# Causal attention and a routed expert layer on one core: masks of one-head score pieces moved from TensorE to VectorE, and the pieces dealt anew among half units

## What is computed

```python
Q, K, V = (proj_split(w, bias) for w, bias in ((q_w, q_b), (k_w, k_b), (v_w, v_b)))
S = jnp.einsum('hid,hjd->hij', K, Q) * SCALE
delta = idx[:, None] - idx[None, :]
S = jnp.where(delta < 0, -jnp.inf, S) - delta          # causal, with a decay
C = jax.nn.softmax(S, axis=-1)
attn = jnp.einsum('hij,hjd->hid', C, V)
...
x = x + (attn @ o_w.T + o_b) * silu(experts(xn))
```

## Time and profile before

| | us |
|---|---|
| median of 3 runs | 805.32 (805.02 to 805.58) |
| the profiled execution | 801.64 |
| its span, first to last instruction | 799.7 |
| PE busy | 746.0 (93%) |
| DVE busy | 534.0 (67%) |
| ACT busy | 520.5 (65%) |
| POOL busy | 245.4 (31%) |

### The profile page before, as it was taken

The page is one execution under the profiler, slowest core; times in us unless marked ns, Lnnn a source line. Parts: engine busy times, 40 slices in busy tenths (PEclk is TensorE's granted clock), DMA queues, the critical chain, the costliest instruction groups (busy, mean ns, idle before and its releaser), DMA issues.

```text
span 799.7 us, 16759 instructions
## 1 busy us (share of the span) xinstructions
PE 746.0 (93%) x5575; PEld 447.8 (56%) x5579; DVE 534.0 (67%) x1084; ACT 520.5 (65%) x1044; POOL 245.4 (31%) x311
## 2 busy tenths in 40 slices
PE   4999998999999999999999999989988999999884
PEld 2555553444554554544544544544437899999763
DVE  2456878788777787787787787787404544444287
ACT  3775556576676676676676676666786566666354
POOL 0442232251123223223223222202134457444300
PEclk9999999999999999999999999999999999999998
DMA  8889935254466476486486476495555765555487
GB/s 206 242 204 270 248 127 126 35 107 96 99 121 122 114 143 131 101 146 134 96 146 141 95 139 138 97 141 115 122 93 163 184 187 170 160 168 164 147 289 248
DMA packets 85253, 119.49 MB, mean 149 GB/s; under 512 B 14175, under 2 KB 58719, under 8 KB 85119
## 3 DMA queue, kind: packets, MB, share of 16 engines
q1 hardware_dynamic: 76654, 94.50, 53.0%
q0 software_dynamic: 8528, 24.07, 9.9%
HBM read 72.61 MB, written 45.52 MB: 148 GB/s over the span
## 4 chain that ended last, share of the span: by engine, by line
PE 66%; DVE 12%; DMA 9%; issue 5%; ACT 3%; SPq 2%; POOL 2%; ACTq 0%; POOLq 0%; DVEq 0%
PE ps L1401 15%; PE ps L1338 13%; PE ps L1387 12%; PE ps L1481 8%; PE ps L1503 7%; DVE mxa L988 7%; DMA arena<-y_dram 3%; PE ps L1390 3%; PE ps L1299 2%; PE ps L1341 2%; PE ps L1464 2%; DMA q_parts<-arena 2%; POOL arena L648 2%; DMA aug<-q_parts 2%; ACT arena L879 1%
## 5 line engine op out<-in xcount | busy, mean ns | idle before, releaser
L988 DVE TENSOR_REDUCE mxa<-ps 128x1 f32<-128x512 f32 (+3 forms) x608 | 363.0, 654 | 93.6 <-PE ps L1341 63.4
L879 ACT ACTIVATE arena<-ps 128x512 f32<-128x512 f32 x576 | 312.1, 604 | 148.5 <-PE ps L1390 130.0
L1338 PE MATMUL ps<-aug 105*128 105x512 bf16 (+3 forms) x768 | 228.8, 327 | 12.8 <-DVE mxa L988 9.5
L1387 PE MATMUL ps<-aug 108*128 108x512 bf16 (+3 forms) x768 | 216.2, 327 | 2.3 <-ACT arena L879 0.8
L1401 PE MATMUL ps<-arena,v_q 128*32 128x512 f32 (+3 forms) x1536 | 140.4, 491 | 3.7 <-ACT arena L879 3.7
L1338 PEld LDWEIGHTS ps<-aug 105*128 105x128 bf16 x768 | 74.8, 98 | 81.9 <-DVE mxa L988 34.6
L1387 PEld LDWEIGHTS ps<-aug 108*128 108x128 bf16 x768 | 66.1, 98 | 84.1 <-issue 32.5
L1390 PE MATMUL ps<-maskT_sb,idb 128*128 128x128 bf16 x512 | 112.4, 220 | 0.0
L1341 PE MATMUL ps<-mask_sb,idb 128*128 128x128 bf16 x512 | 98.6, 219 | 0.0
L764 POOL DMA_INDIRECT xs_dram<-arena,slot x64 | 62.8, 982 | 104.8 <-ACT arena L879 91.0
L785 POOL DMA_INDIRECT y_dram<-arena,y_row_of x71 | 68.8, 969 | 73.2 <-DVE arena L1238 72.1
(11 more groups left out here) (136 smaller groups left out, 670.6 us busy)
## 6 DMA issues: line engine op xcount, KB each, us to landing
aug<-k_parts SPq DMA_DIRECT2D x96, 128.0 KB, 4.7
aug<-q_parts SPq DMA_DIRECT2D x96, 128.0 KB, 5.2
arena<-xs_dram SPq DMA_DIRECT2D x71, 128.0 KB, 2.7
arena<-y_dram SPq DMA_DIRECT2D x16, 512.0 KB, 4.9
k_parts<-arena SPq DMA_DIRECT2D x16, 384.0 KB, 5.9
q_parts<-arena SPq DMA_DIRECT2D x16, 384.0 KB, 4.4
arena<-in_x SPq DMA_DIRECT2D x8, 512.0 KB, 6.2
xn_dram<-arena SPq DMA_DIRECT2D x8, 512.0 KB, 8.1
```

What stands on the lines that cost most here:

```text
L879: nc.scalar.activation(probs[SLOT[k, u]][:, half], score_bank(q, i), ACT.Exp).then_inc(exp_done, 1)
L988: nc.vector.tensor_reduce(mxa[:, h:h + heads, col_], src, AX.X, ALU.max).then_inc(piece_used, 1)
L1338: ins = nc.tensor.matmul(out_, k_aug[n][0:SCORE_ROWS, h0 + h, ib * P:(ib + 1) * P], q_aug[n][0:SCORE_ROWS, h0 + h, lo:lo + width], start=T ...
L1387: ins = nc.tensor.matmul(out_, q_aug[n][0:ALL_ROWS, h, jb * P:(jb + 1) * P], k_aug[n][0:ALL_ROWS, h, i0:i0 + hi - lo], start=True, stop=lo ...
```

## The change

Pieces of one head with the diagonal (blocks 2, 3, 6 and 7: 16 of the 38 pieces of a quad) no longer get their mask by a matmul. VectorE reads the piece, adds a wide mask from SBUF (zeros, then the 128 mask columns), writes the sum back into the bank and takes the maximum, in one call tensor_tensor_reduce. For blocks 6 and 7 the maximum starts from that of the first 512 columns, so two of the four merges in split_maxima go. In the program the call is two instructions: the main one and one that writes the accumulator to mxa.

The items are dealt by a table, ITEMS_AFTER, with 0 to 2 items behind a half unit. Batches follow half units 4 (B4 of the quad before), 9 (B0), 17 (B1), 24 (B2) and 35 (B3), each with one item ahead of it and, where the table has two there, one right behind it. The zeros tile and the mask share one tile (blank), for which the row number in xs_dram moved from the last column to the first.

```diff
-BATCH_STEP = (10, 18, 26, 34, NU + 2)
-EXTRA_ITEM = (6, 14, 30)
+ITEMS_AFTER = (2, 0, 0, 2, 2, 2, 1, 1, 1, 2, 1, 1, 1, 1, 1, 1, 0, 2, 1, 1, 1, 0, 1, 1, 2, 1, 1, 1, 1, 1, 1, 1, 1, 0, 1, 2)
+BATCH_AFTER = (4, 9, 17, 24, 35)
+ITEMS_BEFORE_BATCH = (1, 1, 1, 1, 1)
...
+def masked_by_vector(piece):
+
+    ib, lo, h, heads, width = PIECES[piece]
+    return heads == 1 and lo + width == P * (ib + 1)
...
+MERGED = len({ib for piece, (ib, lo, *_) in enumerate(PIECES) if 0 < lo and not masked_by_vector(piece)})
...
-        zeros = sb("zeros", [P, W])
+        blank = sb("blank", [P, W + P // 2])
+        zeros = blank[:, 1:W]
+        wide_mask = blank[:, :].bitcast(bf16)
+        mask_sb = wide_mask[:, 2 * W:2 * W + P]
...
-                sp.dma_start(xg[j], xs_dram[bass.ts(n, P), 0:D]).then_inc(xg_in[j], 16)
+                sp.dma_start(xg[j], xs_dram[bass.ts(n, P), 1:W]).then_inc(xg_in[j], 16)
...
-                nc.vector.tensor_reduce(mxa[:, h:h + heads, col_], src, AX.X, ALU.max).then_inc(piece_used, 1)
+                if masked_by_vector(piece):
+                    row = banks[:, 0:width]
+                    begin = NEG
+                    if lo > 0:
+                        dve.wait_ge(piece_used, s - HQ + PIECE_BANKS + 1)
+                        begin = mxa[:, h, TB // 2 + ib:TB // 2 + ib + 1]
+                    nc.vector.tensor_tensor_reduce(
+                        out=row, in0=row, in1=wide_mask[:, 2 * W + P - width:2 * W + P], scale=1.0, scalar=begin,
+                        op0=ALU.add, op1=ALU.max, accum_out=mxa[:, h, ib:ib + 1]).then_inc(piece_used, 1)
+                else:
+                    nc.vector.tensor_reduce(mxa[:, h:h + heads, col_], src, AX.X, ALU.max).then_inc(piece_used, 1)
...
-                    diagonal = lo + width == P * (ib + 1)
+                    diagonal = lo + width == P * (ib + 1) and not masked_by_vector(piece)
...
-                pe.wait_ge(m_in, 48 * q + 48)
-                for i in range(NU):
-                    half_unit(q, n, i)
-                    for _ in range(2 if i in EXTRA_ITEM or first and i == COUNTS_STEP else 1):
...
-                    if i in BATCH_STEP:
-                        send_batch(q, n, BATCH_STEP.index(i))
-                    elif NU + i in BATCH_STEP and not first:
-                        send_batch(q - 1, (n - 1) % AUG, BATCH_STEP.index(NU + i))
...
+                pe.wait_ge(m_in, 48 * q + 48)
+                for i in range(NU):
+                    half_unit(q, n, i)
+                    count = ITEMS_AFTER[i] + (first and i == COUNTS_STEP)
+                    if i not in BATCH_AFTER:
+                        send_items(count)
+                        continue
+                    b = BATCH_AFTER.index(i)
+                    send_items(ITEMS_BEFORE_BATCH[b])
+                    if b > 0:
+                        send_batch(q, n, b - 1)
+                    elif not first:
+                        send_batch(q - 1, (n - 1) % AUG, NTY - 1)
+                    send_items(count - ITEMS_BEFORE_BATCH[b])
```

More of the change, by code:

```diff
@@ L68 @@
 PIECE_BANKS = SCORE_BANKS = 3
-assert len(BATCH_STEP) == NTY
+assert len(BATCH_AFTER) == len(ITEMS_BEFORE_BATCH) == NTY and len(ITEMS_AFTER) == NU
 SHARES_STEP = 27
@@ L91 @@
 WIN = len(stream(1))
-assert WIN % PIECE_BANKS == 0 and NU % SCORE_BANKS == 0 and WIN == NU + len(EXTRA_ITEM)
+assert WIN % PIECE_BANKS == 0 and NU % SCORE_BANKS == 0 and WIN == sum(ITEMS_AFTER)
 AUG = 3
@@ L436, in _ @@
                      "wv": (wvg_sb[:, :, 0:D], weights(wvT)), "gate": (wvg_sb[:, :, D:D + E], weights(gate)),
-                     "idb": (idb[:, :], ident_b), "mask": (mask_sb[:, :], mask_neg),
+                     "idb": (idb[:, :], ident_b), "mask": (mask_sb, mask_neg),
                      "maskT": (maskT_sb[:, :], mask_negT), "before": (before_sb[:, :], before),
@@ L638, in _ @@
             pool.sem_inc(split_done, 8)
-            nc.gpsimd.memset(zeros[:, 0:D], 0.0).then_inc(zeros_set, 1)
+            nc.gpsimd.memset(zeros, 0.0).then_inc(zeros_set, 1)
             for n in range(AUG):
@@ L732, in clear_pads @@
                 nc.gpsimd.indirect_dma_start(
-                    out=xs_dram, in_=zeros[:, :], in_offset=None,
+                    out=xs_dram, in_=blank[:, 0:W], in_offset=None,
                     out_offset=bass.IndirectOffsetOnAxis(ap=pad_slot[:, e:e + 1], axis=0)).then_inc(xs_zero, 16)
@@ L753, in _ @@
                 first_tile, count = MOVES[r], MOVES[r + 1] - MOVES[r]
-                pool.dma_start(x_move[:, 0:count, 0:D], xn_t[:, first_tile:first_tile + count, :]).then_inc(x_moved, 16)
+                pool.dma_start(x_move[:, 0:count, 1:W], xn_t[:, first_tile:first_tile + count, :]).then_inc(x_moved, 16)
                 next_v(q, q % AUG)
@@ L758, in _ @@
                     pool.wait_ge(scattered, 16 * (2 * first_tile + k * count))
-                    nc.gpsimd.tensor_copy(x_move[:, 0:count, D:W].bitcast(i32),
+                    nc.gpsimd.tensor_copy(x_move[:, 0:count, 0:1].bitcast(i32),
                                           y_row[:, first_tile:first_tile + count, k:k + 1]).then_inc(rows_ready, 1)
@@ L1046, in _ @@
             ahead_of_windows = iter(list(enumerate(stream(0))))
+            dve.wait_ge(zeros_set, 1)
+            dve.wait_ge(consts_in, 16 * NCONST)
             def next_items(i):
@@ L1340, in send_piece @@
                     if diagonal:
-                        ins = nc.tensor.matmul(out_[:, width - P:], idb[:, :], mask_sb[:, :], start=False, stop=True)
+                        ins = nc.tensor.matmul(out_[:, width - P:], idb[:, :], mask_sb, start=False, stop=True)
                 ins.then_inc(piece_done, 1)
@@ L1419, in window, with send_items @@
                 sent = 0
-                pe.wait_ge(m_in, 48 * q + 48)
-                for i in range(NU):
-                    half_unit(q, n, i)
-                    for _ in range(2 if i in EXTRA_ITEM or first and i == COUNTS_STEP else 1):
+                def send_items(count):
+                    nonlocal sent
+                    for _ in range(count):
                         held = q == NQ - 2 and i < MAXIMA_STEP and sent < len(items) and items[sent][0] == "maxima"
@@ L1452, in _ @@
                 window(q, q % AUG, first_item(q), items_of(q), first=q == 0)
-            for g, step in enumerate(BATCH_STEP):
-                if step >= NU:
-                    send_batch(NQ - 1, (NQ - 1) % AUG, g)
+            send_batch(NQ - 1, (NQ - 1) % AUG, NTY - 1)
             pe.wait_ge(piece_used, LAST_ITEM + PIECE_BANKS)
```

17 lines of the change are left out of this document (7 added, 10 removed).

## The result

The changed kernel takes 793.91 us (792.26 to 795.13, 4 runs), the kernel before 805.17 (802.2 to 805.58) beside it: a ratio of 0.987 with an interval of 0.984 to 0.990. A later repeat gave 0.988 (0.986 to 0.991). The profiled execution took 794.79 us against 801.64, its span 793.0 against 799.7.

The account below looks back on a forecast made before the run. The rhythm of batches, three banks and VectorE was taken to bound the kernel. Saving 0.94 us per window, 10.3 over eleven plain windows plus 0.9, 0.5 and 0.7, gave 12.4 off 805.3: 793 us, range 781 to 817.

Parts of the forecast that it names:

- What bounds the kernel: Between batches, the rhythm of batches, three banks and VectorE sets the window: 29.3 us by count against 29.71 measured.
- What ends the runs to B1 and B3 after the change: VectorE ends both runs, at 5.8 and 7.25 us; TensorE's own work would take 5.54 and 6.95.
- Masks off TensorE: 16 masks of 0.06 us leave TensorE per window, 0.96 us, worth nothing by itself where TensorE waits for VectorE.
- The new reduction: On VectorE, each of 16 pieces costs 0.07 us more without and 0.13 with a starting value, 1.6 us per window.
- The deal: A piece directly behind each batch starts VectorE at 0.42 us instead of 0.70, 1.1 us less idle per window.
- The late load: In the run to B2, the load lets item 24 start 2.65 us after B1, where TensorE would be there at 2.26.
- The 0.4 us carried over as unexplained: Per window, the count gave 29.3 us against 29.71 measured; the missing 0.4 was carried over unchanged.
- The rest of the kernel: Gains of 0.9 us in windows 1 and 2, 0.5 in 14, 0.7 ahead of the windows, none in 0 and 15.
- A: VectorE takes over in the runs to B1 and above all B3: 820 us at the upper price, slower; chance 0.20.
- B: The new reduction costs 0.05 us less, TensorE's work sets B1 and B3: 785 us, 780 with load in time; chance 0.17.
- C: Waits for ScalarE ahead of B0 and B2 and a later load take the gain: 804 to 806 us; chance 0.08.
- D: The new reduction runs at half rate, 0.5 us more each, VectorE needing 32 us per window: 860 us; chance 0.03.

Follow-up runs that it names:

- the two halves of the change: Against the kernel before: the new deal with masks still matmuls, 795.47 us (0.990); the new reduction in the old deal, 811.67 us (1.010).
- the best version: The changed kernel with operand loads issued earlier and the gather of table y_row_of moved from window 13 to 14: 780.14 us, 0.971 of the kernel before.

## Why the prediction was right, point by point

The forecast was 793 us, 12.4 less than before; measured were 793.91 and 11.3 less. The sign and the size hold. Inside, what ends two of the five runs was wrong, and several terms were off in opposite directions; that the median came within 1 us is in part luck. The profiled execution gained only 6.9 us.

- **What bounds the kernel.** Right: 29.09 and 30.11 us per window for the two halves of the change, where the same hand count had given 29.1 and 30.3. In the old deal a run between two batches is ended by VectorE's last bank, and the masks alone made it longer.
- **What ends the runs to B1 and B3 after the change.** Wrong: the count had VectorE end both, at 5.8 and 7.25, and TensorE's own work at 5.54 and 6.95. The last piece ahead of B1 did not wait for VectorE (317.29 against a bank free at 316.95), and with the measured prices VectorE's way there would be 0.43 + 4 x 0.54 + 0.68 + 0.33 + 1.86 = 5.46. TensorE's own work ended that run. It takes 5.72 because each batch starts 0.09 later than the last piece's own cost, which the sum of 28.2 per window leaves out five times; another 0.1 is not accounted for. At B3 no wait for VectorE is named either: TensorE's weight loads name ScalarE, 0.29 at most. The numbers 5.8 and 7.25 were right by luck. In the best version, too, TensorE's own work is nearly the whole window: 28.2 - 0.96 + 5 x 0.09 = 27.7 of 27.9.
- **Masks off TensorE, 0.96 us, "worth nothing by itself" where TensorE waits.** Right: alone they are part of a loss. In the new deal with loads in time TensorE no longer waits there, and they are worth 0.75 us.
- **The new reduction.** Mis-sized: predicted +0.07 and +0.13, 1.6 us per window; measured +0.05 and +0.07, 1.0 us. The starting value costs 0.02, not the 0.06 of the row it was priced by (L965). The accumulator write was to delay the next instruction by 0.07 and the main one to cost no more without a starting value; in the rows the next instruction starts with the write, and the 0.05 lies between the main one's start and the write's. So the sum 0.07 for that form was close with its parts the wrong way round. The rule on held instructions (the Trainium skill, VectorE: DVE Perf Modes, Two Vector instructions with no wait between them) agrees with the rows: the write starts at 320.56 while the instruction that began at 319.89 lasts until 320.65. The Trainium skill (Vector Engine (DVE) Microarchitecture Reference, Measured stream behaviour on trn2) states about 75 ns per instruction. Added once to the plain 0.60, as an estimate, that gives 0.68 for the pair, against 0.65 and 0.67 measured; the rows don't show it as a gap behind the write.
- **The deal.** The runs to B4, B0, B1 and B3 came within 0.1 us of the count. I forecast 0.8 to 0.9 us of idle behind a batch; it is 0.97, 0.82, 1.14 and 0.57 behind B3, B0, B1 and B2 and none around B4, 3.5 us in a window where it had been 6.0 (1.15, 1.15, 1.27, 1.69 and 0.73). The start behind the batch was right, the work in hand at its beginning a little less than thought (1.15 us at B1 instead of 1.4).
- **The late load.** Right in kind, mis-sized: the wait was to be 0.4 us and is 0.5 to 2.1 in most windows, 3 to 4 in window 13, where the table's gather runs. The 5.6 us from issue to use came from one row of a calm window; in the window of the 2.14 us wait it was 7.0 (issued at 258.59), in window 13 8.7.
- **The 0.4 us carried over as unexplained.** That was wrong: with loads in time the windows take 27.9, which the count with the load in time reaches without it. It happened to stand in for the missing lateness: in the window shown the run to B2 is 0.46 longer than forecast, the others together 0.16 shorter, 28.8 forecast, 28.7 measured and 28.8 on average. In the kernel before, the 0.4 stays open; it is spread over B1, B2, B3 and B4 at about 0.1 each.
- **The rest of the kernel.** The forecast for the profiled execution, 789, missed by 6 us. The ten plain stretches from the third B1 to the thirteenth gained 9.5 us, as forecast (9.4). Window 13 took 33.9 us instead of 30.8, with the stall and the fall of the clock, which no term had. The last window took 1.2 us more, and from the last B1 to the end it was 214.5 us instead of 212.3; both are unexplained. Against that, the first two stretches from B1 to B1 gained 2.3 us, where windows 0 to 2 together were forecast at 0.9.
- **The rivals.** A did not happen: the price stayed below, far from the 0.10 above the forecast at which it decides. B had the right price (0.04 less on average) and the right end, TensorE's own work at B1 and B3, but not its gain: that work takes 5.7 and 7.2 us, late load or not, and not 5.54 and 6.95. Its "780 if the load also comes in time" is the time of the best version by luck. C was partly there, by the load. The sign that would have spoken for it showed too, small: ahead of B0 TensorE's weight load names ScalarE (0.23 us, of which the matmul stood 0.11), ahead of B2 nothing is named. D did not happen.

## What to carry to other kernels

Where two engines hand banks to each other in a fixed pattern, add up the pattern between two fixed points of the timeline: this gave the window within 0.3 us in five of six variants, where the busy shares (93% and 67%) did not tell that taking work off TensorE would make the old deal slower. Then ask the trace what ended each run: here two runs had the forecast length and another end, and only that tells why moving the masks pays in the new deal. Work taken off the busiest engine and put on the one that ends the waits can make a kernel slower, and the same move can pay after the order has been changed. When a change moves work forward, look at each transfer released by a fixed step of the program: the distance to its use shrinks and its time to land does not.

## What the runs showed of the hardware

- A VectorE reduction that adds a second operand from SBUF, writes the sum back to PSUM and starts from a value in SBUF takes 0.67 us for 512 columns in a stream, 0.65 without the starting value, the plain reduction 0.60. The write of its accumulator shows 0.14 us in the profile, and the next reduction starts at the same moment as it.
- With a gather of 9088 entries of 4 bytes in flight beside other transfers the DMA share was 1.11 to 1.23 for 11 us at 64 to 93 GB/s, the gather took 20.9 us to land, and a 128 KB load issued more than 10 us ahead still came late. With little beside it the gather took 10.2 us.
- After TensorE had stood for 3 us in the middle of dense work, its granted clock was 0.67 and 0.65 over the next two stretches of 5 us, and whole again behind them. The length of one stall does not tell it: the clock fell to 0.68 behind one of 1.74 us and to 0.66 behind one of 2.20, and stayed whole behind one of 1.80 and one of 1.97.
- A batch of matmuls started 0.31 us after the last piece of 512 columns ahead of it, which costs 0.22 between other matmuls.
